# Four message-passing layers on one core: blocks ranked by length, and the node work of three layers moved into their edge loops

## The reference

```python
h = relu(layernorm(x)); x = x + L0(h)   # attention, 8 heads, self loops, then feed-forward and batch norms
h = relu(layernorm(x)); x = x + L1(h)   # msg = lin1(n2m(h))[src] * (r2m(rbf) * C[:, None]); m2n(lin2(segment_sum(msg, dst)))
h = relu(layernorm(x)); x = x + L2(h)   # attention, 1 head: softmax over the edges of a node, relu(sum of messages)
h = relu(layernorm(x)); x = x + L3(h)   # msg = (h @ W)[src] * norm[:, None]; relu(segment_sum(msg, dst) + b)
```

## Time and profile before

| stage | from, to (us) | length |
|---|---|---|
| setup | 0 to 83.5 | 83.5 |
| n0 | 83.5 to 242 | 158.5 |
| e0 | 242 to 1393 | 1151 |
| rest of layer 0 | 1393 to 1721.8 | 328.8 |
| n1 | 1721.8 to 1795 | 73.2 |
| e1 | 1795 to 2880 | 1085 |
| `filter_out`, n2 | 2880 to 3004 | 124 |
| e2 | 3004 to 4071 | 1067 |
| `gat_out`, n3 | 4071 to 4180 | 109 |
| e3 | 4180 to 5233 | 1053 |
| `gcn_out` | 5233 to 5289 | 56 |

### The profile page before, as it was taken

How to read it: one execution, slowest core, us unless ns; L and a number is a source line. 1 busy time by engine, 2 the same in 40 slices (tenths; PEclk the granted TensorE clock), 3 DMA queues, 4 the chain that set the end, 5 groups by cost and what they waited for, 6 DMA issues and landing times. The chain is left out here.

```text
span 5289.2 us, 84332 instructions
## 1 busy us (share of the span) xinstructions
PE 3685.2 (70%) x13836; PEld 2611.5 (49%) x13837; DVE 3402.8 (64%) x8962; ACT 1876.9 (35%) x5244; POOL 3252.7 (61%) x3433
## 2 busy tenths in 40 slices
PE   6877777777898666666666688777776655555553
PEld 3445555555654544554445555555554444444442
DVE  6588888888834466666666666666667444444445
ACT  1366666666544400000002666666664300000000
POOL 1177777777200377777775277777774477777773
PEclk9977777777898787767888777777777777777776
DMA  2144444444200344444442233333332233333333
GB/s 90 62 129 126 126 127 126 126 126 126 77 21 0 93 115 113 114 115 116 115 116 63 80 105 106 106 106 106 105 106 69 88 105 105 105 105 105 105 105 102
DMA packets 346183, 533.06 MB, mean 101 GB/s; under 512 B 84669, under 2 KB 238346, under 8 KB 346122
## 3 DMA queue, kind: packets, MB, share of 16 engines
q0 software_dynamic: 146432, 386.15, 26.9%
q1 hardware_dynamic: 199690, 146.29, 9.6%
HBM read 502.55 MB, written 29.59 MB: 101 GB/s over the span
## 5 line engine op out<-in xcount | busy, mean ns | idle before, releaser
L677 POOL DMA_INDIRECT e_rows<-table,e_stage x3328 | 3189.8, 958 | 1225.9 <-issue 1098.4
L707 PE MATMUL banks<-e_rows,e_hot 128*128 128x273 f32 (+2 forms) x4992 | 1714.4, 492 | 793.7 <-DMA e_rows<-table,e_stage 439.1
L714 DVE TENSOR_TENSOR acc<-acc,banks 128x273 f32 (+3 forms) x3328 | 1299.8, 391 | 784.2 <-PE banks L707 578.4
L707 PEld LDWEIGHTS banks<-e_rows,e_hot 128*128 128x128 f32 x4992 | 1134.5, 268 | 1056.2 <-issue 493.9
L707 PE MATMUL banks<-e_rows,e_weighted_hot 128*128 128x257 f32 x1664 | 672.9, 544 | 2.1 <-issue 0.3
L815 ACT ACTIVATE e_apart<-const,dst_loc 128x128 bf16<-128x128 f32 x1664 | 507.4, 388 | 0.1
L688 ACT COPY e_stage<-src_idx 128x8 int32 (+1 forms) x416 | 80.4, 196 | 1024.8 <-DMA e_rows<-table,e_stage 985.0
L707 PEld LDWEIGHTS banks<-e_rows,e_weighted_hot 128*128 128x128 f32 x1664 | 389.2, 261 | 92.4 <-issue 25.9
L1258 ACT COPY e_scaledT<-banks 99x384 f32<-99x384 f32 x104 | 49.8, 479 | 1005.4 <-PE banks L1294 1005.4
L497 POOL MEMSET acc<- 128x13377 f32 x3 | 33.7, 11247 | 502.1 <-POOLq L142 419.0
L1373 DVE TENSOR_TENSOR e_rows<-e_rows,banks 128x384 f32<-128x384 f32 (+1 forms) x416 | 155.6, 416 | 227.5 <-DMA e_rows<-table,e_stage 225.3
(11 more groups left out here) (233 smaller groups left out, 4981.3 us busy)
## 6 DMA issues: line engine op xcount, KB each, us to landing
e_edge_in<-in_edge_attr SPq DMA_DIRECT2D x832, 80.0 KB
e_rows<-table,e_stage POOLq DMA_INDIRECT x3328, 2.7
e_node_rows<-node_line SPq DMA_DIRECT2D x104, 256.0 KB, 3.3
table<-n_row SPq DMA_DIRECT2D x49, 132.0 KB, 1.7
table<-n_row SPq DMA_DIRECT2D x49, 129.0 KB, 2.2
X<-in_x SPq DMA_DIRECT2D x1, 6272.0 KB, 23.1
values<-table SPq DMA_DIRECT2D x49, 128.0 KB, 2.0
table<-n_row SPq DMA_DIRECT2D x49, 128.0 KB, 1.7
```

The lines of the kernel that those rows point to most:

```text
L677: nc.gpsimd.indirect_dma_start(out=rows[:, u, q, 0:width], out_offset=None, in_=table, in_offset=bass.IndirectOffsetOnAxis(ap=stage[:, u, ...
L707: nc.tensor.matmul(banks[:, 2 + q % 4, 0:width], onehot, rows, start=True, stop=True).then_inc(summed_tile, 1)
L714: nc.vector.tensor_tensor(at, at, banks[:, 2 + q % 4, 0:width], ALU.add).then_inc(added, 1)
```

## The change

- The setup ranks the blocks by their number of steps, shortest first, and steps go through the blocks in that order. `begun` and PE's pass over it are gone; a chain of small operations on DVE and PE makes the ranks (`ranked`: rank to block), and `pick` is made with one operation for each of the seven groups.
- `filter_out`, n2, `gat_out`, n3 and `gcn_out` are gone as stages. Their work for the block of rank k is done in the edge loop before them, in batches 8+2k and 9+2k, and in part in the two behind (classes FilterNode in e1, GatNode in e2, GcnNode in e3); k runs to 47 in the loops (IN_LOOP = 48), and the last block, which has the most steps, is done after the loop, together with what is left of rank 47. In e3 the block's output is stored by two DMAs.
- An engine that needs the number of the block of rank k loads it into a register (`load_ranked`, one TENSOR_LOAD). In e2 DVE does this once in an even batch and twice in an odd one.
- In e2 the norm's inverse root comes from DVE: a guess (three operations on one column, L2083 to L2087) and three Newton steps of three operations each (L2094 to L2098).
- POOL no longer clears `acc` at the start of n0, n1 and n2: in n0 it copies a zero tile for each block, one clearing stands at the start of `feed_forward`, ACT clears a block in e1 when it has taken it, and in e2 ACT writes the next layer's own row over it.
- Beside these: `plain_edges` has its one-hot ring cut from four batches to two, one bank for the turned scales instead of two, bank 7 for the node work, and the loads of e2's restart flags are issued two batches ahead.

The diff, cut to its core:

```diff
+LAG = 8
+IN_LOOP = (BATCHES - LAG) // 2
+REFINES = 3
+STEPS2 = 5 + 3 * REFINES
...
+def node_turns(nc, engine, body):
+    def ranks(i, r):
+        return (2 * i + r // 2 - LAG // 2) if not isinstance(i, int) or 2 * i + r // 2 >= LAG // 2 else None
+    def turn(i):
+        for r in range(RING):
+            k = ranks(i, r)
+            last = ranks(i, r - 2) if r >= 2 else (ranks(i - 1, r + 2) if not isinstance(i, int) or i else None)
+            body(i * RING + r, r, k, last)
+    for i in range(LAG // RING):
+        turn(i)
+    turn(LAG // RING)
+    with nc.Fori(LAG // RING + 1, TURNS - 1, engines=[engine], head_slot={engine: 0}) as i:
+        turn(i)
+    turn(TURNS - 1)
...
+                    now = step(v.scalar_tensor_tensor(spread[:, 1, :], size_key[0:NB, :], own_size[:, 0:1], ones[0:NB, 0:NB], ALU.is_lt, ALU.mult,
+                                                      accum_out=own_steps[:, 1:2]))
...
+                    now = step(v.tensor_tensor(halves(tile_k), prep_("iota_k").rearrange("p (h k) -> p h k", h=2), banks[:, 2:4, 0:HALF], ALU.add))
...
                     for g in range(GROUPS):
-                        last = v.scalar_tensor_tensor(pick[:, g, :], prep_("iota_k"), first_step[:, 1, g:g + 1], begun[:, g, :], ALU.is_lt, ALU.mult)
+                        v.tensor_scalar(pick[:, g, :], tile_k[:, :], prep_("tile")[:, g:g + 1], None, ALU.is_equal)
...
+                    v.tensor_scalar(ranked[:, :], banks[0:1, 4, 0:NB], 1.0, None, ALU.subtract)
...
-                        if tag != "n3":
-                            nc.gpsimd.memset(acc[:, :, :], 0.0)
+                        if clear:
+                            nc.gpsimd.memset(extra[2][:, :], 0.0).then_inc(cleared, 1)
+                            pool.wait_ge(cleared, 1)
...
+            nc.gpsimd.tensor_copy(acc[:, bass.ds(b, 1), :].squeeze(1), S["extra"][2][:, :])
...
+        def load_ranked(engine, k):
+            return nc.values_load_multi_w_load_instructions(
+                ranked[0:1, bass.ds(k, 1)], engines=[engine], min_val=0, max_val=NB - 1,
+                skip_runtime_bounds_check_because="a block's number")[1][0]
...
+                            if even and k is not None:
+                                node.act_part(act, k, load_ranked(ACT_ENGINE, k))
+                            if even and last is not None:
+                                node.act_norm(act, last, load_ranked(ACT_ENGINE, last))
+                            if not even and last is not None:
+                                node.act_own(act, last, load_ranked(ACT_ENGINE, last))
...
+                            if even and last is not None:
+                                node.act_keep(act, last)
...
+                            if k is not None:
+                                b = load_ranked(DVE_ENGINE, k)
+                            if last is not None and not even:
+                                b_last = load_ranked(DVE_ENGINE, last)
...
+                            if k is not None and not even:
+                                node.dve_add(dve, k, b)
+                            if last is not None and even:
+                                node.dve_refine(dve, last, 2)
+                                node.dve_coefs(dve, last)
                             if more:
                                 all_maxima(j + 1, (r + 1) % 2)
                             add(1)
+                            if k is not None and even:
+                                node.dve_share(dve, k, b, added, j)
+                            if k is not None and not even:
+                                node.dve_stats(dve, k, b)
...
                             add(2)
...
+                            if k is not None and not even:
+                                node.dve_aggregate(dve, k)
                             add(3)
                             if more:
                                 powers(j + 1, un)
...
+                            if k is not None and not even:
+                                node.dve_guess(dve, k)
                             add(4)
                             if still:
                                 value(j + 2, (r + 2) % RING)
+                            if last is not None and not even:
+                                node.dve_row(dve, last, b_last)
                             add(5)
+                            if k is not None and not even:
+                                node.dve_refine(dve, k, 0)
...
                             add(6)
...
+                            if k is not None and not even:
+                                node.dve_refine(dve, k, 1)
                             add(7)
                             if still:
                                 tile_maxima(j + 2, r % 2)
...
+                            for k in range(IN_LOOP - 1, NB):
+                                b = load_ranked(DVE_ENGINE, k)
+                                if k >= IN_LOOP:
...
+                            if first and not filtered:
+                                node.dve_scale(dve, k, b, added, j)
                             add(1)
+                            if filtered and second:
+                                node.dve_add(dve, k, b)
                             if inside(j + 1):
...
+                            if first and not filtered:
+                                node.dve_add(dve, k, b)
...
+                    @blk.gpsimd
+                    def _(pool):
+                        nc.gpsimd.memset(acc[:, :, :], 0.0)
...
+            def dve_scale(self, dve, k, b, added, j):
+                dve.wait_ge(added, j * G + 4)
+                nc.vector.scalar_tensor_tensor(banks[:, 7, 0:D], acc[:, bass.ds(b, 1), 0:D].squeeze(1), dinv[:, bass.ds(b, 1)], banks[:, 7, D:2 * D],
+                                               ALU.mult, ALU.add).then_inc(self.part_ready, 1)
+            def dve_add(self, dve, k, b):
+                dve.wait_ge(self.part_ready, k + 1)
+                dve.wait_ge(self.out_done, 32 * k + 32)
+                at = of_node(X, b)
+                nc.vector.scalar_tensor_tensor(at, banks[:, 7, 0:D], 0.0, at, ALU.max, ALU.add).then_inc(self.updated, 1)
...
+                sp.dma_start(out[bass.ds(b * P, LAST), :], X[0:LAST, bass.ds(b, 1), :].squeeze(1)).then_inc(self.out_done, 16)
+                sp.dma_start(out[bass.ds(c * P + LAST, P - LAST), :], X[LAST:P, bass.ds(c, 1), :].squeeze(1)).then_inc(self.out_done, 16)
...
+            def dve_share(self, dve, k, b, added, j):
+                dve.wait_ge(added, j * G + 4)
+                nc.vector.tensor_scalar(self.share[:, 0:1], acc[:, bass.ds(b, 1), D:D + 1].squeeze(1), 1e-16, None, ALU.add).then_inc(self.den, 1)
+                dve.wait_ge(self.den, k + 1)
+                nc.vector.reciprocal(self.share[:, 1:2], self.share[:, 0:1]).then_inc(self.share_ready, 1)
...
+            def dve_guess(self, dve, k):
+                v, n = nc.vector, self.norm
+                dve.wait_ge(self.steps, STEPS2 * k + 2)
+                v.tensor_scalar(n[:, 2:3], n[:, 1:2], LN_EPS, None, ALU.add).then_inc(self.steps, 1)
+                dve.wait_ge(self.steps, STEPS2 * k + 3)
+                v.tensor_scalar(self.bits[:, 0:1], n[:, 2:3].bitcast(I32), 1, None, ALU.arith_shift_right).then_inc(self.steps, 1)
+                dve.wait_ge(self.steps, STEPS2 * k + 4)
+                v.tensor_scalar(self.bits[:, 1:2], self.bits[:, 0:1], -1.0, float(0x5f3759df), ALU.mult, ALU.add).then_inc(self.steps, 1)
+            def dve_refine(self, dve, k, turn):
+                v, n = nc.vector, self.norm
+                root = self.bits[:, 1:2].bitcast(F32) if turn == 0 else n[:, 4:5]
+                done = STEPS2 * k + 5 + 3 * turn
+                dve.wait_ge(self.steps, done)
+                v.scalar_tensor_tensor(n[:, 5:6], root, n[:, 2:3], root, ALU.mult, ALU.mult).then_inc(self.steps, 1)
+                dve.wait_ge(self.steps, done + 1)
+                v.tensor_scalar(n[:, 5:6], n[:, 5:6], -0.5, 1.5, ALU.mult, ALU.add).then_inc(self.steps, 1)
+                dve.wait_ge(self.steps, done + 2)
+                v.tensor_tensor(n[:, 6:7] if turn == REFINES - 1 else n[:, 4:5], root, n[:, 5:6], ALU.mult).then_inc(self.steps, 1)
+            def dve_coefs(self, dve, k):
+                v, n = nc.vector, self.norm
+                dve.wait_ge(self.steps, STEPS2 * k + STEPS2)
+                v.scalar_tensor_tensor(n[:, 7:8], n[:, 0:1], -1.0, n[:, 6:7], ALU.mult, ALU.mult).then_inc(self.coefs, 1)
...
+            def dve_row(self, dve, k, b):
+                dve.wait_ge(self.product, k + 1)
+                dve.wait_ge(self.stored, 16 * k + 16)
+                dve.wait_ge(self.own_kept, k + 1)
+                nc.vector.tensor_scalar(self.row[:, :], banks[:, 1, D:2 * D], dinv[:, bass.ds(b, 1)], None, ALU.mult).then_inc(self.row_ready, 1)
+            def act_own(self, act, k, b):
+                act.wait_ge(self.row_ready, k + 2)
```

(20 more changed lines are left out.)

692 lines of the change are left out of this document (465 added, 227 removed).

## The result

Four runs of the changed kernel have a median of 5198.77 us (5196.4 to 5199.56), the kernel before 5288.98 (5285.21 to 5289.75): ratio 0.9831, interval 0.9818 to 0.9844. It is faster by 90 us (1.7%) where 151 were forecast (5138). The time lies in the range of 5040 to 5235, but two terms of the sum are far off, one to either side, and partly cancel; that the total lies inside owes something to luck, since one term lies outside its own bounds.

What follows compares the result with a forecast made beforehand. POOL's gathers were taken to bound e1, e2 and e3, with 298 us of gaps around them to win. Savings of 278 us, less 122 in e2 and 5 in e1, gave -151: about 5138 us, range 5040 to 5235.

Steps and rivals of the forecast that it cites:

- The bound before: In the second to fourth edge loops POOL's gathers set the pace, about 10.0 us per batch; other engines wait for rows.
- The gaps: Between loops: e1 to e2 becomes 17 us (-110), e2 to e3 21.5 (-91), the end 7 (-51).
- Clearing of `acc`: In n0 and n1: without POOL's clearing, a held DVE operation on 49 columns gets short, -10 us each.
- The setup: Before the first edge loop: one PE pass goes, 10.3 us, but ranking makes `pick` ready 4.3 us later; -6 us.
- e2: In this loop node work adds 5.4 us per pair; DVE becomes the bound at 11.3 per batch: +122 us.
- the drain rule: In e2: a semaphore costs only the pipeline's drain, so no gaps take node work, 36 us more; not adopted.
- e1: In this loop DVE's spare 4.4 us per pair covers about 2.4 of node work; +5 us, bounds 0 and +40.
- rival B: Handoffs of node work between engines bind: +67 us in e2, +29 in e1, 5234; sign e1 above 10.7; chance 0.18.
- Rival C: In e2 POOL's gathers hold seven DVE operations per pair, mostly Newton's, 0.95 us each: +319, 5457; chance 0.04.
- Rival A: e2 costs less: register loads overlap, small operations start 0.12 us apart; +43 in place of +122, 5059; chance 0.16.
- e0: The first edge loop, which the change does not touch: 0 us.
- e3: The last edge loop: DVE gets a load and two operations of 0.4 us in a batch that waits longer: 0.

Runs made afterwards that it cites:

- experiment 1: In loop e1 of the changed kernel, the one-hot and logit-product operations with two SBUF operands became one-operand reductions of as many elements; 5099.64 us, ratio 0.9629.
- `setup_pick`: The changed kernel with the setup's semaphore raised right behind `pick`, on another chip where the kernel before takes 6638.64 us; ratio 0.9762.

## Why the prediction was right or wrong

**The bound before** was right: e1, e2 and e3 at POOL's rate, and the gaps as the thing to win.

**The gaps** were right in size. Counted as the prediction did, but in e1 from the loop's last addition (2930.6, and 4114.9 in e2), they are 23.8 and 22.9 us for 17 and 21.5, and -50 for -51 at the end (56.5 and now 6.0 from e3's last addition to the end of the span; the prediction's 58.3 run to the end of the execution). In e1's border the last block's chain took 16.2 (2930.6 to 2946.7, its last operation) where I set 10.5. Of the 9 us that e2's gap gave less in the table, -81.6 for -91, 8 are the loop's own end: from last gather to last addition 29.0 us, before 20.9.

**Clearing of `acc`:** -10.2 for -10 at n1; in n0 -8.5 for -10, with 0.43 us for the operation on 49 columns (L508) where I looked for under 0.3. **The setup** gave -1.3 for -6. The pass of PE that goes was worth 10.4 us for 10.3; what failed is "`pick` is ready 4.3 us later". It is ready 6.4 us later (24.6 to 31.0), since the ranking is longer than the 11.6 us I set, and five operations stand between `pick` and the operation that raises its semaphore (3.3 us where it was 0.6), which the kernel shows and I did not read.

**e2** was right in kind: DVE leads, POOL waits, `value` does not. The size was +89 for +122. From 3100 to 4000 a pair takes 22.2 us where the sum had 22.6. Three terms were set too high: a register load of one number is 0.309 and not the 0.598 of the eight numbers in the earlier trace rows, so 1.2 per pair and not 1.8 by the gap ahead of the rescale (0.91 to 1.50 a batch); the other node operations take 3.3 and not 3.6; the loop without its waits 17.0 and not 17.2. A Newton step between additions costs 0.42, where the sum had 0.60 less 0.18, which is right. Against that, the sum took DVE's waits for PE off and left them off; they are 0.76 per pair, and were 0.71 before (27.0 and, ahead of L1052, 5.1 us in 45 pairs). Over the 96 batches the period is 11.0 and not 11.3, which makes +97 from first to last rescale where the gathers show +89. The 0.2 us between additions are filled by node work, as I took from the rows, so the 36 us of the drain rule did not appear.

**e1** is the step that failed: "I add **+5** for waits in order" with bounds of 0 and +40, for +70.6. At 11.0 us per batch it also went over the 10.7 that were to be the sign of rival B; but with every handoff in place experiment 1 brings it to 10.0, so it is not B. I counted DVE's slack (4.4 us in a pair against 2.4) and took a free DVE as cover. The slack was indeed there: DVE still waits 111.3 us for rows from 1900 to 2800, where it waited 193.5. What the node work moved was the moment at which two long operations run, against gathers that start each 1.25 us. Before, DVE waited for a row in each batch and so ran in step with POOL; collisions took 0.3 us per batch. With less waiting they take 1.0. That it is the node work, and not the shorter one-hot ring, that moved the moment was not tried by itself, but the loop's start speaks for it: up to 1878, where the first block's node work begins, the short ring is there already, and the excess is 0.5 us per eight gathers (0.3 in the same 77 gathers before); behind that it is 1.0. The kernel before shows the cause in its own gathers, a mean of 982 ns in e1 and 945 to 957 in the other loops, and I passed over it.

**Rival C** named the right resource and the wrong victim. The Newton operation with one input and SBUF alone on both sides takes 0.154 us (L2096, 121 times, none above 0.155), so no gather holds it. The Trainium skill (SBUF — State Buffer, "Who interferes with whom") also says that a DVE instruction with two SBUF inputs contends with a GpSimd instruction that reads SBUF, by way of its second input; the trace agrees, with 101.9 us in e1, under 2 once both have one input (experiment 1), and none in e3, where the other input is in PSUM. The rule for `tensor_scalar`, which I weighed, is seen in one place: the rescale, 257 columns from SBUF to SBUF. It takes 0.355 us as a rule, but in e2 of the kernel before 31 of 102 start 0.46 to 0.68 us behind the start of a gather and take 0.38 to 0.60; the 0.56 in the earlier trace rows is one of them. That costs 6 us in the whole loop, and 0.2 in the change, where only two fall so. Single columns show nothing of it. **Rival B** (handoffs) had +29 in e1 and +67 in e2; in e1 experiment 1 excludes it, and in e2 DVE's waits for PE are what they were (0.76 per pair for 0.71). **Rival A** was half true: loads of one number are cheaper, but three of them add 1.2 us per pair, so they don't overlap.

## What to carry to other kernels

An engine with slack is cover for more work only if what it already does is harmless at any moment: before moving work onto it, look whether its long operations hold another engine, and at what moment they run against that engine's work now. Cut an operation that holds the engine that sets the pace into short ones; here that cost DVE 44 us of busy time in e1 and made e1 78 us shorter. And price a moved stage against what it takes in the loop: the gap of e2 gave 82 us and the loop took 89.

## What the runs showed of the hardware

- A gather (indirect DMA, issued by GpSimd) that starts during a VectorE operation with two SBUF operands waits until 0.13 us before that ends: up to 0.95 us more than 0.945, in 218 gathers of 832 in e1. The same operation with one of the two in PSUM (e3) holds none of 92. Four operations of 128x256 in a row let it in between: 23 us of excess for 102.
- The other way round, a VectorE `tensor_scalar` of 257 columns from SBUF to SBUF that starts 0.46 to 0.68 us into a gather takes up to 0.60 us and not 0.355 (31 of 102 in e2 before); one on a single column does not.
- A register load takes 0.309 us for one number, 0.535 for two, 0.599 for eight, on DVE's sequencer; 0.279 for one on ACT's and 0.437 on SP's.
- The first pass of 28 matmuls in the setup takes 12.2 to 12.5 us, later ones 10.31 (before, after and `setup_pick`).
- Chips differ: on one of three, the kernel before took 25% longer (6638.64 us) with the same durations on the engines, as gathered rows landed later; there the edits to e1 took no time away.
